# Tables of VectorE's long operations in a PSUM bank, in the ranking and in the gated edge pass

## The reference

```
edge_index = jnp.stack([src, dst])
x = _layernorm(x + relational(x, ...))      # three layers
x = _layernorm(x + gated(x, edge_index, ...))
x = _layernorm(x + attention(x, ...))
x = _layernorm(x + conv(conv(x, ...), ...))
```

```
h = relu(_ln(x @ W1 + b1, g1, bt1))
h_src = h[row]                                            # row, col = src, dst
ef = concatenate([h_src, h[col]], axis=1)
edge_weights = sigmoid(relu(ef @ We1 + be1) @ We2 + be2)[:, 0]
aggr = segment_sum(edge_weights[:, None] * h_src, col, num_segments=n)
```

## Time and profile before

| | us |
|---|---|
| median of 3 runs | 11741.47 (11733.28 to 11742.6) |
| profiled execution | 11709.46 |
| its span, first to last instruction | 11707.7 |
| ranking, first scatter to end of the last | 212 to 1333 of the span |
| gated pass, first gather to end of the last | 6279 to 7459 of the span |

### The profile page before, as it was taken

The page is one execution under the profiler, slowest core; times in us unless marked ns, Lnnn a source line. Parts: engine busy times, 40 slices in busy tenths (PEclk is TensorE's granted clock), DMA queues, the critical chain, the costliest instruction groups (busy, mean ns, idle before and its releaser), DMA issues. The chain is left out here.

```text
span 11707.7 us, 167974 instructions
## 1 busy us (share of the span) xinstructions
PE 8126.2 (69%) x50988; PEld 6507.4 (56%) x50988; DVE 8894.5 (76%) x15409; ACT 4025.8 (34%) x10657; POOL 6805.0 (58%) x7047
## 2 busy tenths in 40 slices
PE   3555257887778887788856777547774788868885
PEld 3444224665446665466645666435653677767774
DVE  8666647898569896698966777578888788758886
ACT  0111123333333333333323555323332344424442
POOL 2777404777137772277734777327773577727773
PEclk8555578888888888888877888767676898879896
DMA  5333475444663446634444888612223577857775
GB/s 192 104 104 104 146 284 199 107 107 106 200 228 108 107 107 178 262 108 107 107 65 157 269 271 273 146 30 56 55 56 36 201 263 265 254 138 264 264 266 146
DMA packets 718027, 1884.83 MB, mean 161 GB/s; under 512 B 265961, under 2 KB 324022, under 8 KB 677736
## 3 DMA queue, kind: packets, MB, share of 16 engines
q0 software_dynamic: 306624, 795.04, 27.0%
q1 hardware_dynamic: 410536, 1079.17, 25.4%
HBM read 1284.44 MB, written 589.18 MB: 160 GB/s over the span
## 5 line engine op out<-in xcount | busy, mean ns | idle before, releaser
L1172 POOL DMA_INDIRECT h<-table,edges_ring x3552 | 3361.1, 946 | 1131.5 <-issue 1039.2
L1172 POOL DMA_INDIRECT edges_rows<-table,edges_ring x1944 | 1857.4, 955 | 598.2 <-issue 579.7
L1347 PE MATMUL bank<-h,edges_onehot 128*128 128x260 f32 (+1 forms) x5312 | 1575.1, 456 | 168.0 <-DVE h L1504 126.6
L1347 PEld LDWEIGHTS bank<-h,edges_onehot 128*128 128x128 f32 x5312 | 1177.4, 254 | 457.9 <-DVE h L1504 230.3
L2645 POOL DMA_INDIRECT rec<-dst,slots x782 | 881.8, 1128 | 434.2 <-issue 238.1
L1458 DVE TENSOR_TENSOR_SCAN bank<-edges_fresh,edges_top,bank 4x1024 f32<-4x1024 bf16 x440 | 1026.6, 2333 | 3.3 <-PE bank L1322 3.3
L1465 DVE TENSOR_TENSOR_SCAN edges_top<-edges_fresh,bank 4x1024 f32<-4x1024 bf16 x440 | 995.1, 2262 | 1.1 <-issue 0.5
L1322 PE MATMUL bank<-ident,edges_score 128*4 128x128 f32 x3520 | 646.1, 346 | 495.7 <-DVE edges_score L1498 494.0
L1391 ACT ACTIVATE edges_narrow_onehot<-edges_onehot 128x1024 bf16<-128x1024 f32 x444 | 469.1, 1057 | 1089.7 <-DVE edges_onehot L1147 1089.7
L1687 PE MATMUL bank<-edges_w_e,edge_score 128*128 128x128 f32 x3520 | 802.9, 316 | 0.0
L1172 POOL DMA_INDIRECT acc<-table,edges_ring x664 | 679.2, 1023 | 208.8 <-issue 193.9
(11 more groups left out here) (459 smaller groups left out, 19251.6 us busy)
## 6 DMA issues: line engine op xcount, KB each, us to landing
table<-x SPq DMA_DIRECT2D x154, 1040.0 KB, 5.5
edge_score<-edge_feat SPq DMA_DIRECT2D x220, 512.0 KB
edges_onehot<-onehot_d SPq DMA_DIRECT2D x220, 512.0 KB, 3.7
table<-h SPq DMA_DIRECT2D x77, 1040.0 KB, 7.3
table<-turn_typed_rows SPq DMA_DIRECT2D x63, 1040.0 KB, 8.1
h<-table,edges_ring POOLq DMA_INDIRECT x3552
onehot_d<-edges_onehot SPq DMA_DIRECT2D x110, 512.0 KB, 4.9
flip_d<-edges_onehotT SPq DMA_DIRECT2D x110, 512.0 KB, 6.0
```

The costliest lines, as they stand in the source:

```text
L1172: pool.indirect_dma_start(out=rows[r][:, j, :], out_offset=None, in_=table, in_offset=bass.IndirectOffsetOnAxis(ap=ring[:, s * ST + j:s * ...
L1347: ins = pe.matmul(sum_b[k % 3], onehot[s][:, j, :], rows[s][:, j, A0:W], start=j == k * GT, stop=j == (k + 1) * GT - 1)
```

## The change

In ranking, VectorE first copies two 128 x 128 tables, `place0` and `earlier`, into the first half of `bank[3]`, and waits for the copies. `make_hot` gets the table of numbers as an argument: counting still hands it `place0` in SBUF, ranking the copy in the bank. `same` reads `earlier` from the bank. The operations are otherwise the same.

In the gated pass, the tables `place1` and `we2` are copied into the second half of `bank[3]` once; the one-hots and the product with `we2` read them there. ScalarE writes `gate` into the second half of `bank[2]`, beside the transposed `rel`, and VectorE weighs the rows from there. The four sums now stand in the first half of `bank[3]`; each `take` waits until all four sums of its superblock are made, and TensorE waits until all four sums of the superblock before are taken before it makes the first.

```
@@ gated_edges
-        dot, gate = p.buffer("dot", (P, ST)), p.buffer("gate", (P, ST))
+        dot = p.buffer("dot", (P, ST))
...
-        sum_b = [g.bank[3][:, at:at + D] for at in (0, D, 512, 512 + D)]
+        sum_b = [g.bank[3][:, k * D:(k + 1) * D] for k in range(GPS)]
+        place_b, we2_b = g.bank[3][:, 512:512 + P], g.bank[3][:, 512 + P:512 + P + D]
+        gate_b = g.bank[2][:, 512 + P:512 + P + ST]
...
                     if k == 0:
                         pe.wait_ge(rows_weighted, o + 1)
-                    if k % 2 == 0:
-                        hold(pe, sums_taken, GPS * (o - 1) + k + 2)
+                        hold(pe, sums_taken, GPS * o)
...
-                        act.activation(gate[:, :], dot[:, :], ACT.Sigmoid, bias=be2[:, 0:1]).then_inc(gate_made, 1)
+                        act.activation(gate_b, dot[:, :], ACT.Sigmoid, bias=be2[:, 0:1]).then_inc(gate_made, 1)
...
                 v.memset(rel[:, ST:ST + 1], 1.0)
+                k.later(v.tensor_copy(place_b, g.place1[:, :]))
+                k.later(v.tensor_copy(we2_b, we2[:, :]))
...
                 def take(o, k, bins):
-                    v.wait_ge(sums_made, GPS * o + k // 2 * 2 + 2)
+                    v.wait_ge(sums_made, GPS * (o + 1))
...
-                    v.tensor_tensor(rh, rh, gate[:, :].unsqueeze(2).to_broadcast([P, ST, D]), ALU.mult
+                    v.tensor_tensor(rh, rh, gate_b.unsqueeze(2).to_broadcast([P, ST, D]), ALU.mult
...
-                    v.scalar_tensor_tensor(ends_of(n), ends_of(n), 0.0, we2[:, :].unsqueeze(1).to_broadcast([P, ST, D]),
+                    v.scalar_tensor_tensor(ends_of(n), ends_of(n), 0.0, we2_b.unsqueeze(1).to_broadcast([P, ST, D]),
...
-                    make_onehot(v, g, b, onehot[b % RING], onehot_made)
+                    make_onehot(v, g, b, onehot[b % RING], onehot_made, place_b)
@@ program (counting and ranking)
-            def make_hot(v, k, s, T):
+            def make_hot(v, k, s, T, numbers):
                 at = bass.ds(k * CH, T)
-                v.tensor_tensor(place_hot[s][:, 0:T, :], place0[:, :].unsqueeze(1).to_broadcast([P, T, P]),
+                v.tensor_tensor(place_hot[s][:, 0:T, :], numbers.unsqueeze(1).to_broadcast([P, T, P]),
                                 place[:, at].unsqueeze(2).to_broadcast([P, T, P]), ALU.is_equal)
                 return v.tensor_tensor(bin_hot[s][:, 0:T, :],
-                                       place0[:, 0:NBINS].unsqueeze(1).to_broadcast([P, T, NBINS]),
+                                       numbers[:, 0:NBINS].unsqueeze(1).to_broadcast([P, T, NBINS]),
...
-                        make_hot(v, k, s, T).then_inc(hot_made, 1)
+                        make_hot(v, k, s, T, place0[:, :]).then_inc(hot_made, 1)
...
+            number_b, earlier_b = bank[3][:, 0:P], bank[3][:, P:2 * P]
...
                     def hot(k, s, T):
                         hold(v, shares_made, k - 1)
                         hold(v, found_taken, k - 1)
-                        make_hot(v, k, s, T).then_inc(hot_made, 1)
+                        make_hot(v, k, s, T, number_b).then_inc(hot_made, 1)
...
                             ins = v.scalar_tensor_tensor(same[:, t, :], dst_row[s][:, t, :],
-                                                         dst_f[:, bass.ds(k * CH + t, 1)], earlier[:, :],
+                                                         dst_f[:, bass.ds(k * CH + t, 1)], earlier_b,
                                                          ALU.is_equal, ALU.mult)
...
+                    v.tensor_copy(number_b, place0[:, :]).then_inc(tables_kept, 1)
+                    v.tensor_copy(earlier_b, earlier[:, :]).then_inc(tables_kept, 1)
+                    v.wait_ge(tables_kept, 2)
                     hot(0, 0, CH)
```

More of the change, by code:

```diff
@@ L2506, in program @@
             slot_i, tile_i, within = tb("slot_i", [P, CH], I32), tb("tile_i", [P, CH], I32), tb("within", [P, CH])
-            chain, hot_made = sem("rank_chain"), sem("rank_hot_made")
+            chain, hot_made, tables_kept = sem("rank_chain"), sem("rank_hot_made"), sem("rank_tables_kept")
+            number_b, earlier_b = bank[3][:, 0:P], bank[3][:, P:2 * P]
             place_flipped, place_kept, shares_made, before_made, found_made, found_taken = (
```

## The result

The kernel after takes 11540.5 us (median of 3 runs, 11530.4 to 11542.2), before 11741.5: 201 us less, ratio 0.9831 (95% interval 0.9817 to 0.9845). The forecast was 11545. The profiled execution took 11542.2 us, with a span of 11540.4.

The account below looks back on a forecast made before the run. GpSimd's chain of indirect DMAs was taken to bound ranking and the gated pass; -132.6 - 69.2 + 5 + 0.5 = -196.3 us gave 11513 against the profiled execution, 11545 against the median, range 11505 to 11635 (chance 0.74).

Parts of the forecast that it names:

- The bound: Ranking and gated pass: GpSimd's chain of indirect DMAs, 0.30 us between them, ends last: 1119.9 and 1176 us.
- The size: Standing of DMA instructions that goes: 132.6 us in ranking's scatters, 69.2 us in the gated pass's gathers.
- three coincidences in the timeline: Two scatters and a gated gather end 0.82 to 0.84 us after a VectorE instruction with both tensors in SBUF.
- rival D: Both stages: DMA instructions stand for another reason and nothing moves, 11741 us; chance 0.03.
- The remainder: Both stages: short operations keeping two SBUF tensors still hold some DMAs; 5 us taken, at worst 55.
- the copies: New table copies cost 0.5 us once before ranking's first scatter, and 0 in the gated pass.
- Bank operands: VectorE instructions reading a bank get no longer: 0 taken, bounds -0.01 and +0.22 us for each `same`.
- Rival C: Ranking: each `same` with a bank costs 0.22 us more, so ranking gains only 30 us: 11647 us; chance 0.08.
- The four sums: Gated pass: waiting for all four sums is covered by 0.68 us, then by 1.7 us of waiting; nothing added.
- Rival A: Gated pass: takes wait for four sums, TensorE's clock falls, the pass grows 302 us: 11916 us; chance 0.05.
- Rival B: Gated pass: its transfers become the bound, so only ranking's 128 us go: 11614 us; chance 0.10.
- the loop of 13.03 us a chunk: Ranking: loop around VectorE and TensorE, next bound after GpSimd's 13.88 us, 0.85 us a chunk behind.

Follow-up runs that it names:

- run 4: Changed kernel, but the compare of the four attention passes reads its table from SBUF: 11615.3 us, ratio 0.9906 to the kernel before.
- 5: Changed kernel, but place_hot and bin_hot in ranking read their table from SBUF again: 11588.7 us, ratio 0.9900 to the kernel before.
- 6: Changed kernel, but `same` in ranking reads its table from SBUF again: 11553.6 us, ratio 0.9871 to the kernel before.
- 8 to 10: Changed kernel, one gated-pass instruction each with both tensors in SBUF: product with we2, product with gate, compare; 11560.0, 11560.5, 11558.1 us.
- run 7: Changed kernel with the reduction over `same` done twice in each chunk of ranking: 11561.2 us, ratio 0.9877 to the kernel before.
- run 3: Kernel before with only the gated pass's four sums put in one bank, takes waiting for all four: 11724.8 us, ratio 0.9998.
- run 8: Changed kernel, but only the gated pass's product with we2 reads both tensors from SBUF: 11560.0 us, ratio 0.9872 to the kernel before.

## Why the prediction was right

1. The bound: GpSimd's chain in both stages. Shown: its instructions got shorter by 133.0 and 69.2 us, its idle time stayed, and the stages got shorter by 129.5 and 67.6 us.

2. The size: 132.6 and 69.2 us were counted as busy time less count times median. Measured 133.0 and 69.2. The median was the right price to take since the larger part of the instructions never stood (579 of 782 scatters, 756 of 880 gathers).

3. The cause, read from three coincidences in the timeline, is shown by runs 4, 5, 6 and 8 to 10, which each put one operand back into SBUF and got the standing back, and by run 7, whose added instruction has one SBUF tensor and made none. Nor were the three cases picked: of the 203 scatters over 0.02 us above the median before, 69 end 0.83 to 0.84 us after `place_hot` and 133 after a `same`. The Trainium skill's rule (SBUF — State Buffer, "Who interferes with whom"), that a VectorE instruction with two SBUF inputs contends with a GpSimd instruction that reads SBUF, agrees with them. The sentence behind rival D, inferred there, that such a `tensor_tensor` leaves descriptor generation alone, is no guide to an indirect DMA as a whole: in the kernel before a scatter took up to 2.32 us, and 1.14 at most after. Which part of the instruction is held, no run separates; that it is the reading of its indices is argued from the 0.1 us that it does before it stands.

4. The remainder: 5 us were allowed for short operations with two SBUF tensors. They made scatters no longer than 1136 ns and gathers no longer than 979, so this was next to nothing; so were the copies (the first scatter starts at 211.0 us, before at 212.4).

5. Bank operands: taken as free, measured shorter by 4 ns (`same`) and 10 ns (compare). Rival C's upper bound of 0.22 us for a `same` is out. Its gain was also reckoned from a chunk of 15.87 us, 13.88 plus the 1.99 of the one chunk read; the stage itself gives 1119.9 / 71 = 15.77, so 23 us and not 30.

6. The four sums: free, by run 3. Rival A is out, and TensorE's granted clock in the gated pass rose from 0.86 to 0.88, not fell. Rival B too: the DMA engines went from 0.84 to 0.89 busy and did not bound the pass.

7. What is next: the loop of 13.03 us a chunk, by run 7, within 0.25 us of its forecast, and the 0.25 are short operations of VectorE that got longer, which the forecast did not have.

The difference of 32 us between the profiled execution and the median was carried over, and that was right: the stage sum of 197 us agrees with the medians, not with the two profiled spans. That the forecast lies within 5 us of the median is in part luck, since runs of one kernel differ by more.

Two expectations of mine behind the prediction failed in size: run 4, for which I had reads fall anywhere, and in run 8 the first theory of equal shares. Neither changes the forecast, which counted the standing as it was and asked for all of it to go.

## What to carry to other kernels

Where GpSimd's chain of indirect DMAs is the bound, compare the mean of one DMA instruction with its median: the difference times the count is what a neighbour on VectorE costs, and a timeline shows which, since in these traces the DMA ends 0.81 to 0.86 us after the neighbour that held it. Give every long VectorE instruction beside it at most one SBUF tensor (a small table or weight copied to a bank once is enough), and all of them at once: a single one that is left cost 43 to 53 of 69 us here, even the compare, which the trace of before showed beside only 5 of the long gathers.

## What the runs showed of the hardware

The price of such an instruction depends on phase, and I had not expected how much. A gather chain of one instruction every 1.25 us beside VectorE instructions of 1.25 us stands about once for a whole series (69 us for three, 43 to 53 for each alone); a compare in the attention passes started at a free phase about half of the time (88 us for 440); `place_hot`, behind a wait for landings, was hit in nearly every chunk (84 us for 71, 1.2 us each).

Short instructions of VectorE get longer beside a scatter too, though they have a single SBUF input. In ranking of the changed kernel a copy of 49 elements and a scalar operation of 11 have medians of 180 and 172 ns and maxima of 397 and 399; below them a scatter and one long `tile_i` beside it:

```profile
L2632 DVE TENSOR_SCALAR tile_i<-slot_i x72: 153/172/399, 209.5 to 1188.4; 128x11 int32<-128x11 int32 x71, 128x1 int32<-128x1 int32 x1
...
L2616 DVE COPY taken_before<-offs x72: 178/180/397, 202.6 to 1177.9; 128x49 f32<-128x49 f32 x72
...
703.53 0.96 POOL L2652 DMA_INDIRECT rec<-dst,slots  x1 [0.31 <-issue]
...
704.15 0.31 DVE L2632 TENSOR_SCALAR tile_i<-slot_i 128x11 int32<-128x11 int32 x1
```

`tile_i` starts 0.62 us into the scatter and ends 0.03 us before it does. So do all 17 of the 144 that are over 60 ns above their median: they start 0.53 to 0.69 us after a scatter did, and end 0.01 to 0.03 us before its end. By these times it is the later part of a scatter that holds them, and not its first 0.1 us, after which a scatter is itself held; what GpSimd does in that part, no run shows, and none tests it. It costs nothing in the changed kernel, since VectorE waits 246 us for landings of scatters anyway, but about 0.3 us a chunk in run 7, where VectorE and TensorE are the bound.

No run points to a version that beats the changed kernel: every operand that was put back made the DMA instructions longer, and what is left in both stages is 0.95 us and 0.30 us of issue for each indirect DMA. Left open is TensorE's idle time near the end of the gated pass (35 us in the changed kernel, where one take waits 32.0 us for it); the profile shows nothing that it waited for.
